# Gated recurrence: the guard of the gates' sum moved from an addition by ScalarE into the logarithm's bias and the refinement

## The chip, the cores and the metric

The kernel runs on one NeuronCore of a Trainium2 chip. The metric is the device time of one execution in microseconds (us), lower is better. Every engine (TensorE = PE, VectorE = DVE, ScalarE = ACT, GpSimd = POOL, SyncE = SP) runs its own list of instructions in order; between engines, and between dependent instructions of one engine, semaphores keep the order.

## What is computed

`x` is 16 sequences of 256 tokens with 256 features, fp32. Four residual layers follow each other: attention, a gated recurrence, a mixture of experts with a shared expert, and a tanh recurrence. The change lies in the second one, which the reference gives as

```python
EPS = 1e-08
forget_gate = sigmoid(x @ W_f.T + b_f)
input_gate = sigmoid(x @ W_i.T + b_i)
gate_sum = forget_gate + input_gate + EPS
forget_norm = forget_gate / gate_sum
input_norm = input_gate / gate_sum
candidate = x @ W_h.T + b_h
new_info = input_norm * candidate
log_ret = log(forget_norm + EPS)
log_cumprod = cumsum(log_ret, axis=1)
padded = concatenate([zeros, log_cumprod], axis=1)
scaling = exp(log_cumprod[:, -1:, :] - padded[:, :-1, :])
hidden = cumsum(scaling * new_info, axis=1)
hidden = hidden + exp(log_cumprod) * cond[:, None, :]
x = x + hidden
```

## The kernel before

`x` lies in SBUF with the features on the partitions (`XT`, 128 partitions x 2 halves of the features x 16 sequences x 256 tokens). The stage before the change is the attention (`attention`), the one after it the experts (`experts`); each is a block of its own, and the next begins when all engines have left the last.

`recurrence` (line 842) works in 16 units, numbered 0 to 15. Unit n is feature half n % 2 of the two sequences of pair n // 2: tiles of 128 x 512. All tiles (`fg`, `ig`, `ie`, `total`, `inv`, `keep`, `start`, `hid`) have two slots, n % 2. Each engine has a written order, and this sets who can wait for whom:

- TensorE (L887): for each unit the products of the input gate, then the forget gate, then the candidate, into the three parts of the PSUM tile `pg`. The candidate of unit n waits until `pn` of unit n - 2 is written (`new_ready`).
- ScalarE, per round: the two sigmoids of unit n + 1 (`ig` L899, `fg` L901), the addition of 1e-8 to the input gate (`ie` L903), a table load (L923), Ln of `total` (L908) and Exp of minus that (L910), which together give a first value of 1 / total in PSUM, a table load back (L911), and then for unit n `keep` = normalised forget gate + 1e-8 (L918). The sigmoid of a unit waits for `keep` two units before it.
- GpSimd, per round: `total` = fg + ie of unit n + 1 (L932), the two normalisations of unit n (`ig` L937, `fg` L938), the two additions to `XT` of unit n - 1 (L945, L947).
- VectorE, per round: `pn` = (candidate + bias) * normalised input gate of unit n (L979), one refinement of the reciprocal of unit n + 1 (L967, L970: with y the first value and s the total, (2 - s * y) * y), then for unit n six scans of 128 x 256 (L989, L991, L995, two each) and the product `hid` (L998). With a cumulative product of `keep` the scans replace the reference's logarithms.

`pn`, `pg` and the zeros of the scans (`pz`) lie in PSUM, the rest in SBUF.

Of the kernel before, what the change touches and what calls it, by code (L numbers as in the profile page):

```python
# [11 lines left out]
P = 128  # L12
# [829 lines left out]
def recurrence(nc, env):  # L842
    fp32, ALU, ACT = (env[k] for k in ("fp32", "ALU", "ACT"))
    sb, ps, sem, vec = (env[k] for k in ("sb", "ps", "sem", "vec"))
    XT, eps8, wfih = (env[k] for k in ("XT", "eps8", "wfih_sb"))
    N = 2 * T
    UNITS = B
    st = ExitStack()
    with st:
        fg = sb(st, "fg", [P, 2, N])  # L850
        ig = sb(st, "ig", [P, 2, N])
        ie = sb(st, "ie", [P, 2, N])
        total = sb(st, "total", [P, 2, N])
        inv = sb(st, "inv", [P, 2, N])
        keep = sb(st, "keep", [P, 2, N])
        after = sb(st, "after", [P, 2, T + 1])
        start = sb(st, "start", [P, 2, N])
        hid = sb(st, "hid", [P, 2, N])
        pg = [ps(st, f"pg{u}", [P, 3, N]) for u in range(2)]
        pn = ps(st, "pn", [P, N])  # L860
        pz = ps(st, "pz", [P, 512])
        constants, products, gates, summed, inverse, normed, kept, new_ready, scanned, hid_ready, added = (
            sem(st, n) for n in ("constants", "products", "gates", "summed", "inverse", "normed", "kept", "new_ready", "scanned",
                                 "hid_ready", "added"))
        i_products, f_products, log_ready, seed_ready, refined = (
            sem(st, n) for n in ("i_products", "f_products", "log_ready", "seed_ready", "refined"))
# [4 lines left out]
        def half(v, j):  # L871

            return v[:, j * T:(j + 1) * T]
# [17 lines left out]
        @block.scalar  # L891
        def _(act):
            def open_gates(n):
                u, q = n % 2, n % 2
                act.wait_ge(i_products, n + 1)
                if n >= 2:
                    act.wait_ge(new_ready, n - 1)
                    act.wait_ge(kept, n - 1)
                nc.scalar.activation(ig[:, q], pg[q][:, 1], ACT.Sigmoid, bias=vec("b_i", u, u + 1)).then_inc(gates, 1)  # L899
                act.wait_ge(f_products, n + 1)  # L900
                nc.scalar.activation(fg[:, q], pg[q][:, 0], ACT.Sigmoid, bias=vec("b_f", u, u + 1)).then_inc(gates, 1)  # L901
                act.wait_ge(gates, 3 * n + 1)
                nc.scalar.activation(ie[:, q], ig[:, q], ACT.Identity, bias=eps8[:, 0:1]).then_inc(gates, 1)  # L903

            def seed(n):
                q = n % 2
                act.wait_ge(summed, n + 1)
                nc.scalar.activation(pg[q][:, 1], total[:, q], ACT.Ln).then_inc(log_ready, 1)  # L908
                act.wait_ge(log_ready, n + 1)
                nc.scalar.activation(pg[q][:, 1], pg[q][:, 1], ACT.Exp, scale=-1.0).then_inc(seed_ready, 1)  # L910
                nc.scalar.preload_act_table_set("sigmoid_and_others")  # L911

            def add_eps(n):
                q = n % 2
                act.wait_ge(normed, 2 * n + 2)
                if n >= 2:
                    act.wait_ge(hid_ready, n - 1)
                nc.scalar.activation(keep[:, q], fg[:, q], ACT.Identity, bias=eps8[:, 0:1]).then_inc(kept, 1)  # L918

            for n in range(-1, UNITS):  # L920
                if n + 1 < UNITS:
                    open_gates(n + 1)
                    nc.scalar.preload_act_table_set("natural_log_exp_and_others")  # L923
                    seed(n + 1)
                if n >= 0:
                    add_eps(n)

        @block.gpsimd
        def _(pool):
            def add_gates(n):  # L930
                pool.wait_ge(gates, 3 * (n + 1))
                nc.gpsimd.tensor_tensor(total[:, n % 2], fg[:, n % 2], ie[:, n % 2], ALU.add).then_inc(summed, 1)  # L932

            def normalise(n):
                q = n % 2
                pool.wait_ge(inverse, n + 1)
                nc.gpsimd.tensor_tensor(ig[:, q], ig[:, q], inv[:, q], ALU.mult).then_inc(normed, 1)  # L937
                nc.gpsimd.tensor_tensor(fg[:, q], fg[:, q], inv[:, q], ALU.mult).then_inc(normed, 1)  # L938

            def add_to_x(n):  # L940
                p, u, q = n // 2, n % 2, n % 2
                pool.wait_ge(hid_ready, n + 1)
                pool.wait_ge(products, 2 * (p + 1))
                xv = XT[:, u, 2 * p:2 * p + 2]
                nc.gpsimd.tensor_tensor(xv, xv, start[:, q].rearrange("p (j t) -> p j t", j=2), ALU.add).then_inc(added, 1)  # L945
                pool.wait_ge(added, 2 * n + 1)
                nc.gpsimd.tensor_tensor(xv, xv, hid[:, q].rearrange("p (j t) -> p j t", j=2), ALU.add).then_inc(added, 1)  # L947

            add_gates(0)
            for n in range(UNITS):  # L950
                if n + 1 < UNITS:
                    add_gates(n + 1)
                normalise(n)
                if n > 0:
                    add_to_x(n - 1)
            add_to_x(UNITS - 1)

        @block.vector
        def _(dve):
            nc.vector.memset(zeros, 0.0).then_inc(constants, 1)  # L960
            nc.vector.memset(after[:, :, T:T + 1], 1.0).then_inc(constants, 1)
            dve.wait_ge(constants, 2)

            def invert(n):
                q = n % 2
                dve.wait_ge(seed_ready, n + 1)
                nc.vector.scalar_tensor_tensor(out=inv[:, q], in0=total[:, q], scalar=-1.0, in1=pg[q][:, 1],  # L967
                                               op0=ALU.mult, op1=ALU.mult).then_inc(refined, 1)
                dve.wait_ge(refined, n + 1)
                nc.vector.scalar_tensor_tensor(out=inv[:, q], in0=inv[:, q], scalar=2.0, in1=pg[q][:, 1],  # L970
                                               op0=ALU.add, op1=ALU.mult).then_inc(inverse, 1)

            def new_info(n):
                u, q = n % 2, n % 2
                dve.wait_ge(products, n + 1)
                dve.wait_ge(normed, 2 * n + 1)
                if n > 0:
                    dve.wait_ge(hid_ready, n)
                nc.vector.scalar_tensor_tensor(out=pn[:], in0=pg[q][:, 2], scalar=vec("b_h", u, u + 1), in1=ig[:, q],  # L979
                                               op0=ALU.add, op1=ALU.mult).then_inc(new_ready, 1)  # L980

            def scans(n):

                p, u, q = n // 2, n % 2, n % 2
                s = Steps(dve, scanned, 6 * n)
                dve.wait_ge(kept, n + 1)
                dve.wait_ge(new_ready, n + 1)
                for j in range(2):
                    s.op(nc.vector.tensor_tensor_scan(half(pn[:], j), half(pn[:], j), half(keep[:, q], j), 0.0, ALU.add, ALU.mult))  # L989
                for j in range(2):  # L990
                    s.op(nc.vector.tensor_tensor_scan(after[:, j, T - 1::-1], half(keep[:, q], j)[:, ::-1], zeros, 1.0, ALU.mult, ALU.add))  # L991
                if n >= 2:
                    dve.wait_ge(added, 2 * (n - 1))
                for j in range(2):
                    s.op(nc.vector.tensor_tensor_scan(half(start[:, q], j), half(keep[:, q], j), zeros, h0[:, u, 2 * p + j:2 * p + j + 1],  # L995
                                                      ALU.mult, ALU.add))
                dve.wait_ge(scanned, 6 * n + 4)
                nc.vector.tensor_tensor(hid[:, q].rearrange("p (j t) -> p j t", j=2), pn[:].rearrange("p (j t) -> p j t", j=2),  # L998
                                        after[:, :, 1:T + 1], ALU.mult).then_inc(hid_ready, 1)

            invert(0)
            for n in range(UNITS):
                new_info(n)
                if n + 1 < UNITS:
                    invert(n + 1)
                scans(n)
# [608 lines left out]
```

## Time and profile before

| | |
|---|---|
| median of 3 runs | 1357.46 us (1354.88 to 1358.3) |
| the profiled execution | 1354.25 us, its span 1352.5 us |
| PE busy | 1215.1 us (90%) |
| DVE busy | 883.2 us (65%) |
| ACT busy | 632.5 us (47%) |
| POOL busy | 329.9 us (24%) |

Times in views are us from the start of the span. In the timeline a row is an instruction (or several alike, xcount): its start, its duration, engine, line, operation, output and inputs, and in brackets the idle time of its engine ahead of it with what ended it. Idle time under about 0.2 us isn't printed. The recurrence lasts from 453.3 us (first product) to 573.9 us (first instruction of the experts).

### The profile page before, as it was taken

To read this page: it belongs to the slowest core of one execution; us is meant where nothing else is said; L and a number is where in the kernel's file an instruction comes from. 1 tells how busy PE (TensorE), PEld (TensorE's weight loads), DVE (VectorE), ACT (ScalarE), POOL (GpSimd) and SP (SyncE) were. 2 spreads that over 40 slices of the span, in tenths; PEclk is the share of its full clock that TensorE was granted. 3 is DMA by queue.
4 is the path that set the end of the run, shared out by engine and by line. 5 is a ranking of instruction groups with operands and counts; after the bars stand their busy time and mean duration, and the time that the engine had idled before them with its cause. 6 is when DMAs were issued, how large, how long until landed. Compare 5 with 4: busy or idle time off the path is not lost. (4 is left out here: it accounts for less than half of the span.)

```text
span 1352.5 us, 34667 instructions
## 1 busy us (share of the span) xinstructions
PE 1215.1 (90%) x14232; PEld 977.0 (72%) x14232; DVE 883.2 (65%) x2091; ACT 632.5 (47%) x1191; POOL 329.9 (24%) x311
## 2 busy tenths in 40 slices
PE   4389999999998888329999999999999999999995
PEld 2257676766665333129999999999988888888884
DVE  4978787887864399867666666666555555555552
ACT  2167777777766599612333333333233333333331
POOL 1554544444453299800000000000000000000000
PEclk9799999999999899759999999999999999999996
DMA  9212121211214000039999999999700000000000
GB/s 348 94 48 95 48 95 49 85 59 64 80 49 148 24 0 1 0 129 397 397 374 366 364 364 365 367 365 364 273 2 18 10 19 11 19 10 19 11 18 18
DMA packets 81196, 188.31 MB, mean 139 GB/s; under 512 B 4112, under 2 KB 14480, under 8 KB 80784
## 3 DMA queue, kind: packets, MB, share of 16 engines
q1 hardware_dynamic: 81040, 186.11, 38.1%
q8 instruction: 113, 1.85, 0.6%
q14 instruction: 43, 0.35, 0.1%
HBM read 160.66 MB, written 25.17 MB: 137 GB/s over the span
## 5 line engine op out<-in xcount | busy, mean ns | idle before, releaser
L1118 ACT ACTIVATE g<-ph,b 128x256 f32<-128x256 f32 x256 | 121.2, 474 | 248.3 <-PE ph L1282 248.3
L549 DVE TENSOR_REDUCE mx<-pR 128x4 f32<-128x1024 f32 x128 | 156.3, 1224 | 62.6 <-PE pR L707 61.2
L1499 DVE STREAM_TRANSPOSE preT<-pr 128x64 f32<-128x64 f32 x256 | 63.7, 249 | 163.7 <-PE pr L1392 163.2
L1280 PE MATMUL ph<-xhi,w 128*128 128x256 f32 x512 | 145.8, 285 | 13.2 <-DMA w<-weight_halves 13.2
L1226 DVE CAST ghi<-g 128x256 fp32r<-128x256 f32 x256 | 74.7, 292 | 126.6 <-ACT g L1118 126.4
L1474 ACT ACTIVATE hs<-preT 128x32 f32<-128x32 f32 x256 | 58.7, 229 | 199.6 <-DVE preT L1499 198.6
L1296 PE MATMUL py<-ghi,w 128*128 128x256 f32 x512 | 145.7, 285 | 1.7 <-DVE glo L1228 1.6
L1281 PE MATMUL ph<-xlo,w 128*128 128x256 f32 x512 | 145.7, 285 | 0.0
L1282 PE MATMUL ph<-xhi,w 128*128 128x256 f32 x512 | 145.7, 284 | 0.0
L1297 PE MATMUL py<-glo,w 128*128 128x256 f32 x512 | 144.9, 283 | 0.0
L1298 PE MATMUL py<-ghi,w 128*128 128x256 f32 x512 | 144.9, 283 | 0.0
L421 ACT ACTIVATE probs<-pR 128x1024 f32<-128x1024 f32 x128 | 129.3, 1024 | 22.6 <-PE pR L716 21.0
L1392 PE MATMUL pr<-wh_sb,hs 128*32 128x64 f32 x4096 | 114.0, 231 | 8.9 <-ACT hs L1474 8.9
L1228 DVE TENSOR_TENSOR glo<-g,ghi 128x256 fp32r<-128x256 f32 x256 | 108.9, 425 | 8.8
L1280 PEld LDWEIGHTS ph<-xhi,w 128*128 128x128 f32 x512 | 99.1, 193 | 13.5 <-issue 13.5
L1543 POOL TENSOR_TENSOR staged<-xc,hs 128x256 f32<-128x256 f32 x32 | 22.7, 732 | 347.5 <-ACT hs L1474 347.5
L1392 PEld LDWEIGHTS pr<-wh_sb,hs 128*32 128x32 f32 x4096 | 71.4, 112 | 46.1 <-ACT hs L1474 13.4
L887 PE MATMUL pg<-XT,wfih_sb 128*128 128x512 f32 x192 | 86.4, 600 | 17.1 <-DVE pn L979 15.9
L1296 PEld LDWEIGHTS py<-ghi,w 128*128 128x128 f32 x512 | 98.2, 192 | 3.4 <-DVE glo L1228 3.2
L1534 POOL MEMSET hs<- 128x2048 f32 x1 | 1.8, 1804 | 403.0 <-POOLq L1049 403.0
L1281 PEld LDWEIGHTS ph<-xlo,w 128*128 128x128 f32 x512 | 99.1, 194 | 0.0
L1282 PEld LDWEIGHTS ph<-xhi,w 128*128 128x128 f32 x512 | 99.1, 194 | 0.0
(195 smaller groups left out, 2973.0 us busy)
## 6 DMA issues: line engine op xcount, KB each, us to landing
w<-weight_halves SPq DMA_DIRECT2D x132, 1024.0 KB, 7.9
weight_halves<-wparts SPq DMA_DIRECT2D x40, 512.0 KB, 3.9
modw<-in_ew SPq DMA_DIRECT2D x32, 256.0 KB, 4.6
xn<-in_x_tok SPq DMA_DIRECT2D x4, 1024.0 KB, 11.7
XT<-in_x_dm SPq DMA_DIRECT2D x2, 2048.0 KB, 14.8
out_dm<-staged SPq DMA_DIRECT2D x16, 256.0 KB, 2.1
modw<-in_sw SPq DMA_DIRECT2D x8, 256.0 KB, 4.0
modw<-in_mod_w SPq DMA_DIRECT2D x1, 768.0 KB, 7.0
```

Source lines behind the costliest of these rows:

```text
L421: nc.scalar.activation(probs[:, j % 4], pR[k][:], ACT.Exp, scale=HD ** -0.5).then_inc(free[k], 1)
L549: nc.vector.reduce_max(mx[:, :, 2 * j:2 * j + 2].rearrange("p t s -> p s t"), pR[k][:].rearrange("p s (t k) -> p s t k", t=TC), AX.X).then ...
L887: i = nc.tensor.matmul(pg[n % 2][:, g], wfih[:, c, g * D + u * P:g * D + (u + 1) * P], XT[:, c, 2 * p:2 * p + 2], start=(c == 0), stop=(c ...
L1118: nc.scalar.activation(g[:, t % RING], ph[t % RING][:, 0:T], ACT.Gelu_apprx_tanh, bias=b1[:, n, f:f + 1]).then_inc(gelu_done, 1)
L1228: nc.vector.tensor_tensor(glo[:, t % RING], g[:, t % RING], ghi[:, t % RING].bitcast(fp32), ALU.subtract).then_inc(lo_done, 1)
L1280: nc.tensor.matmul(dst, whi, hi, start=(k == 0), stop=False)
L1281: nc.tensor.matmul(dst, whi, lo, start=False, stop=False)
L1282: i = nc.tensor.matmul(dst, wlo, hi, start=False, stop=(k == DC - 1))
L1296: nc.tensor.matmul(dst, whi, hi, start=(f == 0), stop=False)
L1297: nc.tensor.matmul(dst, whi, lo, start=False, stop=False)
L1298: i = nc.tensor.matmul(dst, wlo, hi, start=False, stop=(f == FC - 1))
L1392: i = nc.tensor.matmul(dst[QW * j:QW * (j + 1)], prev[:, c], quad(wh[:, c], j), start=False, stop=(c == DC - 1), skip_group_check=True)
```

## The change

Three edits. The addition by ScalarE (`ie`) goes, with its tile, and the guard 1e-8 is put where the sum is used: as the bias of Ln, an operand of 128 x 1 in the place of the plain 0, and as the scalar that is added to `total` in the first half of the refinement. GpSimd adds `fg` and `ig` and waits for two increments of `gates` per unit instead of three. Since the refinement's first half then has no place for the minus sign, it comes out as (s * y - 2) * y, the negative reciprocal; normalised `ig`, `fg`, `pn` and `hid` change their sign, `keep` takes it back by a scale of -1, and the last addition becomes a subtraction. The order on every engine is otherwise unchanged, and so is the number of instructions on TensorE, VectorE and GpSimd; ScalarE has 16 fewer.

```diff
@@ recurrence
-        ie = sb(st, "ie", [P, 2, N])
@@ open_gates(n), ScalarE
                 act.wait_ge(f_products, n + 1)
                 nc.scalar.activation(fg[:, q], pg[q][:, 0], ACT.Sigmoid, bias=vec("b_f", u, u + 1)).then_inc(gates, 1)
-                act.wait_ge(gates, 3 * n + 1)
-                nc.scalar.activation(ie[:, q], ig[:, q], ACT.Identity, bias=eps8[:, 0:1]).then_inc(gates, 1)
@@ seed(n), ScalarE
-                nc.scalar.activation(pg[q][:, 1], total[:, q], ACT.Ln).then_inc(log_ready, 1)
+                nc.scalar.activation(pg[q][:, 1], total[:, q], ACT.Ln, bias=eps8[:, 0:1]).then_inc(log_ready, 1)
@@ add_eps(n), ScalarE
-                nc.scalar.activation(keep[:, q], fg[:, q], ACT.Identity, bias=eps8[:, 0:1]).then_inc(kept, 1)
+                nc.scalar.activation(keep[:, q], fg[:, q], ACT.Identity, bias=eps8[:, 0:1], scale=-1.0).then_inc(kept, 1)
@@ add_gates(n), GpSimd
-                pool.wait_ge(gates, 3 * (n + 1))
-                nc.gpsimd.tensor_tensor(total[:, n % 2], fg[:, n % 2], ie[:, n % 2], ALU.add).then_inc(summed, 1)
+                pool.wait_ge(gates, 2 * (n + 1))
+                nc.gpsimd.tensor_tensor(total[:, n % 2], fg[:, n % 2], ig[:, n % 2], ALU.add).then_inc(summed, 1)
@@ add_to_x(n), GpSimd
-                nc.gpsimd.tensor_tensor(xv, xv, hid[:, q].rearrange("p (j t) -> p j t", j=2), ALU.add).then_inc(added, 1)
+                nc.gpsimd.tensor_tensor(xv, xv, hid[:, q].rearrange("p (j t) -> p j t", j=2), ALU.subtract).then_inc(added, 1)
@@ invert(n), VectorE
-                nc.vector.scalar_tensor_tensor(out=inv[:, q], in0=total[:, q], scalar=-1.0, in1=pg[q][:, 1],
-                                               op0=ALU.mult, op1=ALU.mult).then_inc(refined, 1)
+                nc.vector.scalar_tensor_tensor(out=inv[:, q], in0=total[:, q], scalar=1e-8, in1=pg[q][:, 1],
+                                               op0=ALU.add, op1=ALU.mult).then_inc(refined, 1)
                 dve.wait_ge(refined, n + 1)
                 nc.vector.scalar_tensor_tensor(out=inv[:, q], in0=inv[:, q], scalar=2.0, in1=pg[q][:, 1],
-                                               op0=ALU.add, op1=ALU.mult).then_inc(inverse, 1)
+                                               op0=ALU.subtract, op1=ALU.mult).then_inc(inverse, 1)
```

## Rows read from the trace of the kernel before

**Rows 1.** Steady stretch: length, busy PE, PEld, DVE, ACT, POOL, PEclk, DMA share, GB/s.
```profile
500.00:533.00 33.00, 27.09 (x60) 10.99 (x60) 31.10 (x51) 31.65 (x41) 30.99 (x26) 1.00 0.00 0
```

**Rows 2.** Timeline of ScalarE, one round (sigmoids of unit 14, `keep` of unit 13).
```profile
547.38 0.72 ACT L918 ACTIVATE keep<-fg,eps 128x512 f32<-128x512 f32 x1
548.22 0.69 ACT L899 ACTIVATE ig<-pg,small 128x512 f32<-128x512 f32 x1
548.80 0.68 ACT L901 ACTIVATE fg<-pg,small 128x512 f32<-128x512 f32 x1
549.37 0.72 ACT L903 ACTIVATE ie<-ig,eps 128x512 f32<-128x512 f32 x1
550.11 1.28 ACT L923 ACT_TABLE_LOAD   x1
551.47 0.60 ACT L908 ACTIVATE pg<-total 128x512 f32<-128x512 f32 x1
552.10 0.58 ACT L910 ACTIVATE pg<-pg 128x512 f32<-128x512 f32 x1
552.70 1.28 ACT L911 ACT_TABLE_LOAD   x1
554.00 0.72 ACT L918 ACTIVATE keep<-fg,eps 128x512 f32<-128x512 f32 x1
```

**Rows 3.** Timeline of GpSimd, the round that begins with `total` of unit 15.
```profile
556.78 1.26 POOL L932 TENSOR_TENSOR total<-fg,ie 128x512 f32<-128x512 f32 x1 [0.34 <-ACT ie L903]
558.01 1.26 POOL L937 TENSOR_TENSOR ig<-ig,inv 128x512 f32<-128x512 f32 x1
...
563.01 1.26 POOL L937 TENSOR_TENSOR ig<-ig,inv 128x512 f32<-128x512 f32 x1
```

**Rows 4.** Timeline of VectorE, from `pn` of unit 13 to the last `hid`.
```profile
552.77 0.76 DVE L979 SCALAR_TENSOR_TENSOR pn<-pg,small,ig 128x512 f32<-128x512 f32 x1 [0.34 <-POOL ig L937]
...
559.37 0.76 DVE L979 SCALAR_TENSOR_TENSOR pn<-pg,small,ig 128x512 f32<-128x512 f32 x1 [0.33 <-POOL ig L937]
560.03 0.68 DVE L967 SCALAR_TENSOR_TENSOR inv<-total,pg 128x512 f32<-128x512 f32 x1
560.75 0.69 DVE L970 SCALAR_TENSOR_TENSOR inv<-inv,pg 128x512 f32<-128x512 f32 x1
561.36 1.28 DVE L989 TENSOR_TENSOR_SCAN pn<-pn,keep 128x256 f32<-128x256 f32 x2
...
564.98 0.66 DVE L998 TENSOR_TENSOR hid<-pn,after 128x512 f32<-128x512 f32 x1
565.79 0.76 DVE L979 SCALAR_TENSOR_TENSOR pn<-pg,small,ig 128x512 f32<-128x512 f32 x1
...
570.27 0.66 DVE L998 TENSOR_TENSOR hid<-pn,after 128x512 f32<-128x512 f32 x1
```

**Rows 5.** Timeline of the first two units, ScalarE, and the first `pn` of VectorE.
```profile
457.60 0.71 ACT L903 ACTIVATE ie<-ig,eps 128x512 f32<-128x512 f32 x1
...
463.36 0.72 ACT L903 ACTIVATE ie<-ig,eps 128x512 f32<-128x512 f32 x1
...
466.76 0.76 DVE L979 SCALAR_TENSOR_TENSOR pn<-pg,small,ig 128x512 f32<-128x512 f32 x1 [4.35 <-POOL ig L937]
```

**Rows 6.** Timeline of TensorE, a candidate product of the recurrence.
```profile
553.58 1.98 PE L887 MATMUL pg<-XT,wfih_sb 128*128 128x512 f32 x4 [1.20 <-DVE pn L979]
```

**Rows 7.** Waits in the recurrence: who waited for whom, us in total, times, longest.
```profile
POOL total L932 <- ACT ie L903: 29.6, 16, 18.0
```

**Rows 8.** Busy time and clock by stretch (columns as in rows 1), start of the experts.
```profile
604.00:606.00 2.00, 2.00 (x10) 1.77 (x9) 0.57 (x2) 1.71 (x3) 0.00 (x0) 0.50 1.01 375
606.00:608.00 2.00, 1.76 (x13) 1.49 (x12) 1.76 (x9) 0.55 (x2) 0.00 (x0) 1.00 1.05 420
```

**Rows 9.** Durations (ns, min/median/max) of one line of VectorE and one of GpSimd.
```profile
L989 DVE TENSOR_TENSOR_SCAN pn<-pn,keep x32: 671/683/699, 468.7 to 567.3; 128x256 f32<-128x256 f32 x32
L945 POOL TENSOR_TENSOR XT<-XT,start x16: 1257/1272/1286, 474.4 to 571.0; 128x512 f32<-128x512 f32 x16
```

## The prediction

> **What bounds the stage now.** I first read the busy time by stretch: in the steady part of the recurrence ScalarE (31.65 of 33 us), VectorE (31.10) and GpSimd (30.99) are all nearly full, TensorE is not [rows 1]. Three engines at 94 to 96% can't be told apart by busy time, so I went on to the timelines, to see which one never waits. On ScalarE a round takes 554.00 - 547.38 = 6.62 us and no row shows a wait [rows 2]. GpSimd waits 0.34 us per round, and what ends the wait is `ie` of ScalarE, the instruction that the change removes [rows 3]. VectorE waits 0.33 us per round for the normalised `ig` of GpSimd [rows 4], TensorE 1.20 us for `pn` of VectorE [rows 6]. So the chain of waits runs TensorE <- VectorE <- GpSimd <- ScalarE, and ScalarE's own order closes the loop. From the first `pn` at 466.76 to the fifteenth (unit 14) at 559.37 [rows 5, 4] there are 14 rounds of 6.615 us.
>
> **What a round would take without ScalarE.** The gain is not what ScalarE loses, but the distance to the next bound. Each engine's own round can be read:
>
> - ScalarE: starts of `fg`, `ie` and the table load are 0.57 and 0.74 us apart [rows 2]. Without `ie` the load follows `fg` (0.68 us long) as it followed `ie`, 0.02 us after its end, so 0.70 us after `fg` started instead of 1.31: 0.61 us less, taken as 0.60. `total` can start earlier by the same. ScalarE's round is then 6.0 us.
> - GpSimd: after unit 15's `total` (556.78) it runs five operations without a wait, up to the next `ig` at 563.01 [rows 3], where no `total` stands any more. That is `total`, `ig`, `fg` and two additions, just a round's worth: 6.23 us.
> - VectorE: `pn` of unit 15 starts with no printed wait. At that point GpSimd's `ig` had been finished since 563.01 + 1.26 = 564.27, and ScalarE's work of the unit was over, so this is VectorE on its own: 565.79 - 559.37 = 6.42 us [rows 4, 3]. The round is that long although the idle time taken away is 0.33 us (6.615 - 0.33 would be 6.28), because `hid` ends at 565.64 and `pn`, which also waits for it, starts 0.15 us later, whereas earlier this gap lay hidden in the wait.
> - TensorE: idle for 1.20 of 6.62 us, so 5.42 us.
>
> The longest is VectorE's 6.42. So the round falls from 6.615 to 6.42, by 0.195 us, and not by 0.60.
>
> **The change part by part.**
>
> 1. `ie` removed, steady part: 14 rounds x 0.195 = **-2.73 us**. The other 0.4 us of each `ie` becomes idle time of ScalarE. What is late next is VectorE itself; GpSimd and ScalarE then run ahead of it until the wait for `hid` (`add_to_x`) or for `pn` (the sigmoids) holds them.
> 2. `ie` removed, fill: ahead of the first `pn` stands `total` of unit 1, because GpSimd adds the gates of unit 1 before it normalises unit 0. On the way there ScalarE works through both units alone, so both `ie` (457.60 and 463.36) count whole [rows 5]: 2 x 0.60 = **-1.20 us**.
> 3. The bias of Ln. The trace has no Ln with such an operand. Nearest rows: Ln without it 0.60, Exp 0.58, the sigmoids with one 0.68 and 0.69 (they too have one end in PSUM), the identity with one, SBUF on both ends, 0.72 [rows 2]. So it costs 0 to 0.12 us per Ln; I take 0.09, since the sigmoids are the nearest. In the steady part it is covered: ScalarE's round of 6.09 us, with 0.12 even 6.12, is under 6.42. In the fill Ln of unit 0 lies on the path (**+0.09**), and Ln of unit 1 delays `keep` of unit 0, which ends just as the scans are due: in unit 13, which stands for unit 0 here, `keep` ends at 554.00 + 0.72 = 554.72 [rows 2], and the scans follow `pn` by 561.36 - 559.37 = 1.99 us, thus 552.77 + 1.99 = 554.76 [rows 4]: **+0.09**. In later rounds VectorE is the slower of the two, and `keep` is early. The bounds are 0 and 0.24 for both together. ScalarE: Activation LUTs, section What ACT_TABLE_LOAD costs, in the Trainium skill, prices a bias operand of 128 x 1 at about 93 ns against an immediate one. With that price the sum would be -3.74 instead of -3.75; no row here shows it for an Ln.
> 4. Refinement: an add in the place of a multiply (L967), a subtract in the place of an add (L970). L970, which has an add, takes 0.69, L967 with two multiplies 0.68 [rows 4]: between 0 and +0.01 x 16, **0**. The bound of 0.16 us matters as VectorE is the new bound.
> 5. Scale -1 on `keep` (Exp has such a scale and takes 0.58 [rows 2]), a subtraction on GpSimd instead of an addition: **0**. Their cover, if they cost 0.1 us each, is the 0.3 us that ScalarE and the 0.2 us that GpSimd have left per round.
> 6. After the recurrence the two additions of unit 15, the hand-over to the experts, the gating, the fetch of the experts' weights and their products follow from the last `hid`. Nothing in them depends on absolute time, so they move forward whole: **0**, with one reserve. TensorE enters the experts at a granted clock of 0.50 (1.2 GHz), after it had been idle for most of the time since 555.6 us, and has 1.00 (2.4 GHz) from 606 on [rows 8]. Where this change falls could shift against the work; I allow ±1 us, half of a row of 2 us at either side.
>
> Sum: -2.73 - 1.20 + 0.18 = **-3.75 us**. The profiled execution, 1354.25 us around a span of 1352.5, would go to 1350.5. It stands 3.2 us below the median of the runs, 1357.46; applied to the median the sum gives 1353.7 us. That is 0.28% less, and a measurement of this kernel can tell about 0.3% (4.1 us) from no change.
>
> **The rivals.**
>
> - **GpSimd is the next bound, not VectorE.** If the 0.15 us between `hid` and `pn` belonged to the end of the stage alone, VectorE's round would be near 6.28 and GpSimd's is 6.23, so the round 6.25 or so. For it: ordinary gaps of VectorE are smaller (560.03 + 0.68 to 560.75 is 0.04 us [rows 4]). Against it: unit 15 has the same instructions in the same order. 14 x 0.365 + 1.02 = 6.1 us: 1351.3. Chance 0.12.
> - **ScalarE's addition was not on the loop.** The 1.2 us of the fill comes, but the loop is held by something beside it (the load and the wait for `keep`, for example), so that rounds stay at 6.6: gain 1.0 us, 1356.5. Against it: the wait of GpSimd ended by `ie` in all 16 rounds [rows 7]. Chance 0.10, with the case that the change costs in Ln what it saves.
> - **The experts start at an unlucky moment of the clock.** The gain is halved, 1355.5. Chance 0.12.
> - **Slower: GpSimd and VectorE get into each other's way.** Now both run against each other in fixed phase. After the change GpSimd drifts ahead of VectorE until the wait for `hid` stops it, and other pairs of operations meet. If one VectorE instruction per round had to wait for a whole GpSimd operation (1.27 us), the round would be 6.42 + 1.27 = 7.69 and the stage 14 x 1.075 - 1.0 = 14 us longer: 1371.5. It decides from 0.27 us per round on, where gain and loss cancel. Against it: in the steady part both are busy 94% of the time, thus overlap in nearly every instruction, and the 32 scans still take 671 to 699 ns, the 16 additions 1257 to 1286 [rows 9]. Chance 0.03. SBUF — State Buffer, section Who interferes with whom, in the Trainium skill, says that a VectorE instruction with two SBUF inputs and a GpSimd instruction that reads SBUF exclude each other for their whole length. Here every VectorE instruction of the round has one input in PSUM, so by that rule the rival would not come, and the narrow durations agree.
>
> **How the numbers follow.** Chance of the forecast (round set by VectorE, 6.3 to 6.45 us) 0.63, GpSimd 0.12, no loop gain 0.10, clock 0.12, slower 0.03. The predicted time is the forecast's, 1353.7 us. The unknown costs give it -0.2 to +0.3, the clock ±1. The range goes down to the GpSimd case with some scatter, 1350.5, and up to the case without a loop gain, 1357.0; beyond it are the slow case and the edges of the others. The forecast lies just short of 4.1 us, so with its scatter of about 1 us and a median that moves as much, I give it 0.28 of faster by over 0.3% and 0.35 of within; the GpSimd case is faster, 0.12; the two cases with a lesser gain are within, 0.20 of 0.22; the slower one is slower. Faster 0.41, within 0.3% 0.56, slower 0.03.
>
> **What would show it.** In the timeline of the changed kernel: no `ie`; starts of `fg` and of the table load 0.70 us apart; first `pn` about 1.1 us earlier than 466.76 where the recurrence starts at the same time; rounds of 6.42 us from `pn` to `pn` with no printed wait ahead of `pn`; ScalarE waiting some 0.3 us per round for `pn` or for GpSimd in the later units; Ln at 0.69; TensorE idle for about 1.0 us. The forecast is wrong if the round is below 6.3 or above 6.5, if durations of VectorE or GpSimd grow, or if the time from the last `hid` to the end of the span differs from 1352.5 - 570.93 = 781.6 us [rows 4] by more than 1 us.

## The result and the profile after

| | before | changed |
|---|---|---|
| median of 22 runs | 1358.8 us (1354.88 to 1363.58) | 1355.2 us (1351.15 to 1359.61) |
| ratio to before, 95% interval | | 0.9972 (0.9959 to 0.9985) |
| profiled execution, its span | 1354.25, 1352.5 | 1353.02, 1351.2 |
| recurrence, from ScalarE's first table load to the experts' first VectorE instruction | 453.26 to 573.97: 120.71 | 457.90 to 574.62: 116.72 |
| ahead of it | 453.26 | 457.90 |
| behind it | 778.53 | 776.58 |

The change saves 0.28% of the time by the ratio, which is 3.8 us, with an interval from 0.15 to 0.41% (2.0 to 5.6 us); the medians differ by 3.6 us. A single execution doesn't show that well: the two profiled spans differ by 1.3 us only. Cut at the borders of the stage they do. The recurrence is 3.99 us shorter; the attention ahead of it, whose code is the same in both, took 4.64 us longer in this execution, and what lies behind 1.95 us less. Where those two come from is told at the end; for the change only the stage counts.

The timeline of VectorE in the changed kernel, where line numbers are three lower than before (`pn` is L976, the refinement L964 and L967, `hid` L995), begins with the first two `pn`:

```profile
470.27 0.76 DVE L976 SCALAR_TENSOR_TENSOR pn<-pg,small,ig 128x512 f32<-128x512 f32 x1 [3.73 <-POOL ig L934]
...
476.77 0.76 DVE L976 SCALAR_TENSOR_TENSOR pn<-pg,small,ig 128x512 f32<-128x512 f32 x1
...
501.58 0.66 DVE L995 TENSOR_TENSOR hid<-pn,after 128x512 f32<-128x512 f32 x1
502.39 0.76 DVE L976 SCALAR_TENSOR_TENSOR pn<-pg,small,ig 128x512 f32<-128x512 f32 x1
503.06 0.68 DVE L964 SCALAR_TENSOR_TENSOR inv<-total,pg 128x512 f32<-128x512 f32 x1
503.77 0.69 DVE L967 SCALAR_TENSOR_TENSOR inv<-inv,pg 128x512 f32<-128x512 f32 x1
...
508.80 0.76 DVE L976 SCALAR_TENSOR_TENSOR pn<-pg,small,ig 128x512 f32<-128x512 f32 x1
```

Where [rows 4] had `0.34 <-POOL ig` ahead of each `pn`, nothing is printed now: VectorE shows no wait for another engine (a wait under about 0.2 us would not be printed; `dve_more` below settles it). Its round is 508.80 - 502.39 = 6.41 us (6.405 over 14 rounds) instead of 6.615, the duration of the refinement is as before, and `hid` to `pn` is 0.81 us from start to start, as it was ahead of unit 15 only. The first round is longer, 6.50.

ScalarE's timeline of the same stretch answers to [rows 2]:

```profile
502.70 0.72 ACT L915 ACTIVATE keep<-fg,eps 128x512 f32<-128x512 f32 x1
503.54 0.69 ACT L898 ACTIVATE ig<-pg,small 128x512 f32<-128x512 f32 x1
504.12 0.68 ACT L900 ACTIVATE fg<-pg,small 128x512 f32<-128x512 f32 x1
504.82 1.28 ACT L920 ACT_TABLE_LOAD   x1
506.34 0.69 ACT L905 ACTIVATE pg<-total,eps 128x512 f32<-128x512 f32 x1 [0.23 <-POOL total L929]
507.06 0.58 ACT L907 ACTIVATE pg<-pg 128x512 f32<-128x512 f32 x1
```

`ie` is gone, the load starts 0.70 us after `fg`, Ln takes 0.69 instead of 0.60, and ScalarE now waits for GpSimd's sum. GpSimd in turn runs ahead of VectorE at first. Its sums start 6.26 us apart up to 511.31, and 6.40 us apart from there on, where the addition of `start` follows the end of `hid` by 0.08 us (515.06 and 515.14):

```profile
498.78 1.27 POOL L929 TENSOR_TENSOR total<-fg,ig 128x512 f32<-128x512 f32 x1
505.04 1.27 POOL L929 TENSOR_TENSOR total<-fg,ig 128x512 f32<-128x512 f32 x1
...
549.73 1.27 POOL L929 TENSOR_TENSOR total<-fg,ig 128x512 f32<-128x512 f32 x1
556.13 1.26 POOL L929 TENSOR_TENSOR total<-fg,ig 128x512 f32<-128x512 f32 x1
```

So this trace shows both rounds at once: GpSimd's own, 6.26 us, and VectorE's, 6.405. Four of the waits of the recurrence in the changed kernel, whole stage (who waited for whom, us in total, times, longest); the view names no `ie` and no repeated wait on VectorE:

```profile
POOL total L929 <- ACT fg L900: 24.8, 3, 18.5
PE pg L886 <- DVE pn L976: 12.4, 13, 1.0
ACT pg L905 <- POOL total L929: 4.1, 13, 0.4
DVE pn L976 <- POOL ig L934: 3.7, 1, 3.7
```

### The profile page after: what moved, and what is told of

It is laid out like the page before. It is cut to its first block and busy times, and to the rows that moved or that the text cites. A ratio compares the mean times of both kernels' runs of the same rounds, so it can differ in the third digit from the quotient of the medians.

```text
span 1351.2 us, 34651 instructions
## 1 busy us (share of the span) xinstructions
PE 1219.9 (90%) x14232; PEld 979.4 (72%) x14232; DVE 883.0 (65%) x2091; ACT 624.3 (46%) x1175; POOL 330.0 (24%) x311
## 5 line engine op out<-in xcount | busy, mean ns | idle before, releaser
L1294 PEld LDWEIGHTS py<-glo,w 128*128 128x128 f32 x512 | 98.4, 192 | 0.0
```

The lines of the kernel that those rows point to most:

```text
L1294: nc.tensor.matmul(dst, whi, lo, start=False, stop=False)
```

## The experiments

The stage's length, its first `pn` (counted from the table load that opens it) and its rounds are read from one profile each. They repeat well: `pe_order`, which differs from the changed kernel only in the order of TensorE's products, gave the same 116.72 us, and the first `pn` came at 12.37 in five profiles. (`split_adds` is the exception and is explained there; `before` and the changed kernel both had TensorE at a granted clock of 1.00 in the first 4 us of the stage.) The time of an execution wanders by some 4 us to either side, so the stage is the measure except where a ratio is given.

| kernel | first pn | round | stage |
|---|---|---|---|
| before | 13.50 | 6.615 | 120.71 |
| changed | 12.37 | 6.405 | 116.72 |
| ie_back | 12.90 | 6.63 | 120.91 |
| ie_back_waited | 13.58 | 6.705 | 122.15 |
| exp_bias | 12.45 | 6.405 | 116.87 |
| dve_more | 12.37 | 6.62 | 119.94 |
| pool_more | 12.37 | 6.41, from the sixth on 6.50 | 117.71 |
| pe_order | 12.37 | 6.405 | 116.72 |
| in_place | 12.37 | 6.17, from the fourth on 6.255 | 114.20 |
| split_adds | 13.87 | 6.17 | 114.15 |

### Was ScalarE the loop? ie_back and ie_back_waited

```diff
 # ie_back, against the changed kernel: ie computed, read by nobody
                 nc.scalar.activation(fg[:, q], pg[q][:, 0], ACT.Sigmoid, bias=vec("b_f", u, u + 1)).then_inc(gates, 1)
+                act.wait_ge(gates, 2 * n + 1)
+                nc.scalar.activation(ie[:, q], ig[:, q], ACT.Identity, bias=eps8[:, 0:1])
 # ie_back_waited, against ie_back: the sum waits for it
-                act.wait_ge(gates, 2 * n + 1)
-                nc.scalar.activation(ie[:, q], ig[:, q], ACT.Identity, bias=eps8[:, 0:1])
+                act.wait_ge(gates, 3 * n + 1)
+                nc.scalar.activation(ie[:, q], ig[:, q], ACT.Identity, bias=eps8[:, 0:1]).then_inc(gates, 1)
...
-                pool.wait_ge(gates, 2 * (n + 1))
+                pool.wait_ge(gates, 3 * (n + 1))
```

> The addition ie is put back on ScalarE alone, in its old place between the sigmoids and the table load; nothing reads it, GpSimd's sum doesn't wait for it, and the rest of the change stays. If ScalarE's own order was the loop (the prediction's reading), its round is 6.62 us of before plus 0.09 for the bias of Ln: rounds of 6.70 to 6.71 us from pn to pn, no wait on ScalarE, GpSimd waiting for ScalarE again, first pn at 13.5 + 0.1 us after the table load that opens the stage less what the early sum saves (none: the sigmoid of unit 1 is late by ie of unit 0; ie of unit 1 isn't in the way), so 13.0. Rival, that what held the kernel was only GpSimd's wait for ie: rounds stay at 6.41.

Measured: rounds of 6.63, first `pn` 12.90. The first round was longer, 7.04, since the scans of unit 0 waited 0.5 us for `keep`, which `ie` of unit 1 had delayed. The rival (6.41) is out: with `ie` on ScalarE alone the stage is as long as before (120.91 us against 120.71). But 6.63 isn't 6.70, so ScalarE's own order was not quite the loop. Its timeline shows what differs:

```profile
508.74 0.72 ACT L903 ACTIVATE ie<-ig,eps 128x512 f32<-128x512 f32 x1
509.46 1.28 ACT L923 ACT_TABLE_LOAD   x1
510.76 0.69 ACT L908 ACTIVATE pg<-total,eps 128x512 f32<-128x512 f32 x1
```

Here Ln follows the load by 510.76 - (509.46 + 1.28) = 0.02 us. In [rows 2] it is 551.47 - 551.39 = 0.08, too short for a printed wait: Ln waited for GpSimd's sum, which could only start after `ie`. That gave the second kernel:

> As ie_back, which had rounds of 6.63 us, but GpSimd's sum waits for ie again, as before the change. Theory now: the loop of before wasn't ScalarE's order alone, it went from ie over GpSimd's sum (0.06 + 1.27 + 0.04 us) to Ln, 0.07 us longer than the table load beside it (1.28 + 0.03); so 6.615 = 6.54 + 0.07, and 6.63 = 6.54 + 0.09 of Ln's bias. Then rounds are 6.70 here. Rival, that the sum plays no part and the bias costs nothing in a round: 6.63 again.

Measured: 6.705. VectorE waits 0.34 us in each round, as before the change, and GpSimd 0.41 instead of 0.34. So the loop of before ran `ig`, `fg`, `ie`, over GpSimd's sum, Ln, Exp, load, `keep`. ScalarE's order by itself comes to 6.54 us. No kernel ran with it alone; it is 6.63 less the 0.09 of Ln's bias, and also 6.615 less the 0.07 that the way over the sum is longer than the load, and the two agree. The first `pn` at 13.58 also settles the fill: `ie` of unit 0 on ScalarE delayed it by 0.53 us (`ie_back`), and the wait for both `ie` by another 0.68, 1.21 us together.

### The price of the bias: exp_bias

```diff
-                nc.scalar.activation(pg[q][:, 1], pg[q][:, 1], ACT.Exp, scale=-1.0).then_inc(seed_ready, 1)
+                nc.scalar.activation(pg[q][:, 1], pg[q][:, 1], ACT.Exp, bias=eps8[:, 0:1], scale=-1.0).then_inc(seed_ready, 1)
```

> The changed kernel with the same 128x1 operand as bias of Exp as well (1e-8 is added to the exponent). Ln went from 602 to 692 ns with it. Theory: Exp goes from 582 to about 672 ns, ScalarE's round from about 6.09 to 6.18, which VectorE's 6.405 still covers: rounds of 6.405, the first pn 0.09 us later, and keep of unit 0 another 0.09 behind the scans that need it: stage longer by 0.15 to 0.2 us in all. Rival, that ScalarE has no room left: rounds grow by 0.09, the stage by 1.4 us.

One line of ScalarE in the changed kernel (Ln) and one in this (Exp), durations in ns, min/median/max:

```profile
L905 ACT ACTIVATE pg<-total,eps x16: 691/692/693, 463.7 to 557.4; 128x512 f32<-128x512 f32 x16
```

```profile
L907 ACT ACTIVATE pg<-pg,eps x16: 662/662/664, 463.2 to 557.1; 128x512 f32<-128x512 f32 x16
```

Ln went from 602 to 692 ns, Exp from 582 to 662. Rounds stayed at 6.405; the first `pn` came 0.08 later and the first round took 6.58 instead of 6.50: the stage is 0.15 us longer in all. So the operand costs 0.08 to 0.09 us each time, and in the steady part it is covered. The first round of the changed kernel, 0.095 longer than the others, is the same effect of Ln's bias: `keep` of unit 0 is late by it.

### Which engine is the bound now: dve_more and pool_more

```diff
 # dve_more, VectorE, in each round ahead of scans(n)
+                nc.vector.memset(spare[:], 0.0)
 # pool_more, GpSimd, in each round ahead of the wait of add_gates(n)
+                nc.gpsimd.memset(spare[:, n], 0.0)
```

> The changed kernel with one more VectorE instruction per round, a memset of a spare 128x256 tile in SBUF ahead of the scans (a memset of that size into PSUM took 0.27 us). Theory, VectorE is the bound in every round: rounds grow by the start to start time of the new instruction, 0.20 to 0.27 us, to 6.60 to 6.68, and the stage by 3 to 4 us. Rival, GpSimd or a loop through it is the bound: rounds grow by 0.15 us less than the instruction, or not at all.

Measured: rounds of 6.62. The memset lasts 0.27 us and each round grows by 0.22, as expected for VectorE as the bound; the rival, with GpSimd as the bound, expected 0.15 us less than the instruction. Only the first round grows less (6.50 to 6.62), because there the scans had to wait for `keep` anyway.

> The changed kernel with one more GpSimd instruction per round, a memset of a spare 128x256 tile ahead of the sum (by the kernel's other memsets, 204 ns for 128x128 and 1804 for 128x2048, about 0.3 us). Theory: GpSimd's own round is 6.25 to 6.26 and has 0.15 us of room under VectorE's 6.405; with 0.27 to 0.31 us more it becomes the bound, rounds of 6.52 to 6.57, VectorE waiting for it ahead of pn again. Rival, that GpSimd is covered by more than that: rounds stay at 6.41.

Measured: four rounds of 6.40 to 6.41 after the first, then 6.50 to 6.52. GpSimd's timeline:

```profile
558.75 0.31 POOL L929 MEMSET spare<- 128x256 f32 x1
559.02 1.26 POOL L931 TENSOR_TENSOR total<-fg,ig 128x512 f32<-128x512 f32 x1
```

The memset lasts 0.31 us, but the sum follows it 0.27 us later and the round grew to 6.50, a little less than expected. With 0.10 us per round above VectorE's 6.405, GpSimd first uses up the lead it had, and then holds `pn` up. With its own round of 6.26 in the changed kernel it stood 0.15 us per round under VectorE, and the next gain on VectorE ends there.

### Taking VectorE's gap away: in_place and pe_order

In `in_place`, `pn` is written over the candidate in `pg`, so `new_info` needs no wait for `hid` of the unit before; TensorE has to compute the candidate later.

```diff
 # VectorE
-                if n > 0:
-                    dve.wait_ge(hid_ready, n)
-                nc.vector.scalar_tensor_tensor(out=pn[:], in0=pg[q][:, 2], ...
+                nc.vector.scalar_tensor_tensor(out=pg[q][:, 2], in0=pg[q][:, 2], ...
 # scans and hid read pg[q][:, 2] in the place of pn
 # TensorE
+            for n in range(UNITS + 1):
+                if n < UNITS:
+                    product(n, 1, i_products)
+                    product(n, 0, f_products)
+                if n > 0:
+                    product(n - 1, 2, products)
 # product(n, 2) waits for hid_ready n - 1 (pe_order: new_ready n - 1, as before)
```

> The changed kernel with pn written over the candidate in pg instead of into a bank of its own, so that new_info needs no wait for hid of the unit before; TensorE computes the candidate of a unit after the input and forget products of the next one, and waits for hid two units before. Theory, that the gap of 0.15 us between hid and pn is this wait: pn starts about 0.6 us after hid instead of 0.81, VectorE's own round falls to 6.2, GpSimd's 6.25 to 6.26 becomes the bound: rounds of 6.26, stage shorter by 14 x 0.15 = 2.1 us against the changed kernel, 0.15% of the time. Rival, that the gap is something else (PSUM, the end of a strided operation): rounds stay at 6.41. Second rival: the later candidate products hold pn up: rounds above 6.41.

Measured: ratio to the kernel before 0.9939 (0.9916 to 0.9961). That interval still touches the changed kernel's (0.9959 to 0.9985), so the further gain rests on the stage. The stage is 114.20 us, 2.5 us shorter than the changed kernel's. VectorE's timeline:

```profile
501.86 0.66 DVE L998 TENSOR_TENSOR hid<-pg,after 128x512 f32<-128x512 f32 x1
502.44 0.75 DVE L979 SCALAR_TENSOR_TENSOR pg<-pg,small,ig 128x512 f32<-128x512 f32 x1
```

Without the wait `pn` starts 0.58 us after `hid` and overlaps its end, where it was 0.81. VectorE's own round is 6.17 (second and third round); from then on GpSimd sets it at 6.255. The expectation counted 0.15 us for fourteen rounds; the first three, in which GpSimd still had its lead, gained 0.23 each, hence 2.5 and not 2.1.

> The changed kernel with the in-place variant's order on TensorE alone (candidate products of a unit after the input and forget products of the next), pn in its own bank and the wait for hid ahead of it kept. Theory, that the gain of the in-place variant (rounds 6.25, early ones 6.17) came from the wait for hid: rounds stay at 6.405. Rival, that it came from TensorE's order: rounds of 6.25.

Measured: rounds of 6.405, stage 116.72, first `pn` 12.37. TensorE's order changes nothing by itself, so the gain is that of `pn` in place. That takes the wait away and also lets `pn` be written to another PSUM tile; a kernel with only the wait gone wasn't run, so that it is the wait, and not the tile, is argued and not shown apart.

### Relieving GpSimd too: split_adds

```diff
 # GpSimd, against in_place: add_to_x taken apart (VectorE's waits for free slots of start and hid likewise)
+            def add_start(n):
+                pool.wait_ge(scanned, 6 * (n + 1))
+                ...
+            def add_hid(n):
+                pool.wait_ge(hid_ready, n + 1)
+                pool.wait_ge(start_added, n + 1)
+                ...
                 normalise(n)
-                if n > 0:
-                    add_to_x(n - 1)
-            add_to_x(UNITS - 1)
+                if n > 1:
+                    add_hid(n - 2)
+                if n > 0:
+                    add_start(n - 1)
+            add_hid(UNITS - 2)
+            add_start(UNITS - 1)
+            add_hid(UNITS - 1)
```

> The in-place variant (rounds 6.25) with GpSimd's two additions to XT taken apart: start is added when its scans are done, hid one round later, so that no addition waits for the one just ahead of it (gap of 0.13 us per round), and of the tail behind the last hid only one addition remains instead of two. Theory: GpSimd's round falls to 6.12, VectorE's own 6.17 to 6.18 becomes the bound, 12 rounds x 0.08 = 1.0 us, and the tail 1.35 us: stage 2.3 us shorter than the in-place variant's 114.2 us. Rival, that GpSimd isn't the bound there: only the tail's 1.35 us.

Measured: ratio to the kernel before 0.9943 (0.9922 to 0.9963), not to be told from `in_place`. The rounds are 6.17 as expected, so GpSimd was the bound in `in_place`. The tail was wrong: from the last `pn` to the experts it is 7.66 us instead of 8.17, a gain of 0.5 and not 1.35. GpSimd's timeline at the end:

```profile
569.00 1.26 POOL L948 TENSOR_TENSOR XT<-XT,start 128x512 f32<-128x512 f32 x1 [1.62 <-DVE start L1005]
570.41 1.26 POOL L955 TENSOR_TENSOR XT<-XT,hid 128x512 f32<-128x512 f32 x1
```

The addition of `start` waits for its scans, which end only one VectorE instruction ahead of `hid`, so the addition of `hid` still queues behind it. From the first `pn` to the experts `split_adds` takes 100.28 us, `in_place` 101.83. That its whole stage is no shorter comes from the first `pn`, 1.50 us later in this execution, though the edit leaves the order of everything ahead of it as it was. The first sigmoid waited 2.25 us for TensorE's products, in the changed kernel 0.75 (table load at 457.87 and 457.90):

```profile
461.40 0.69 ACT L904 ACTIVATE ig<-pg,small 128x512 f32<-128x512 f32 x1 [2.25 <-PE pg L885]
```

```profile
459.94 0.69 ACT L898 ACTIVATE ig<-pg,small 128x512 f32<-128x512 f32 x1 [0.75 <-PE pg L886]
```

In the first 2 us of the stage TensorE was granted 0.50 (1.2 GHz) in `split_adds` and 1.00 (2.4 GHz) in all the other nine profiles. Over the longer stretch around it, in `split_adds` and in the changed kernel (columns as in [rows 1]; only TensorE's matter):

```profile
450.00:462.00 12.00, 8.93 (x18) 5.13 (x19) 2.13 (x6) 2.47 (x3) 0.00 (x0) 0.54 0.01 1
```

```profile
450.00:462.00 12.00, 8.89 (x22) 5.18 (x23) 2.17 (x6) 2.90 (x4) 0.00 (x0) 0.71 0.01 1
```

## Why the prediction was right

It gave -3.75 us, 1353.7 us and a chance of 0.56 for a difference within 0.3%; measured were -3.8 us by the ratio (-3.6 by the medians), 1355.2 us and 0.28%. The median is above the forecast because that of the kernel before, with more runs, was 1358.8 and not 1357.46. That the totals meet to 0.1 us is luck, as the interval goes from 2.0 to 5.6 us. What bears the prediction out is the stage, -3.99 us, part by part:

1. Steady part, -2.73 forecast. Against 14 rounds of 6.615 and one of 6.42 (99.03 us) stand one of 6.50 and 14 of 6.405 (96.17 us): -2.86, which already holds the +0.09 of `keep` of unit 0. Without it -2.95. The rest, 0.2 us, is that VectorE's own round is 6.405, while the one round that showed it before was 6.42. The choice to take the round of unit 15, and not 6.615 less the printed idle time (6.28), decided the forecast: 6.28 would have given 2 us more.
2. Fill, -1.20 + 0.09 forecast, measured 12.37 - 13.50 = -1.13. Right to 0.02 us, and for the reason given: the two `ie` put back cost 1.21 us (13.58 - 12.37).
3. Bias of Ln, 0.09 per Ln taken between 0 and 0.12: 602 to 692 ns. ScalarE: Activation LUTs, section What ACT_TABLE_LOAD costs, in the Trainium skill, gives about 93 ns for such an operand. The trace agrees for Ln (90 ns); Exp, with 80 ns, is a little below.
4. Refinement, sign and subtraction, 0: VectorE's 0.68 and 0.69 stand, and GpSimd's operations take 1.26 to 1.28 as before.
5. Tail of the stage, 0: 8.18 us from the last `pn` to the experts in both.

**What it had wrong.** The sentence that ScalarE's own order closes the loop: the loop ran over GpSimd's sum, and ScalarE alone was 6.54 us (worked out from `ie_back`). Hence ScalarE's round after the change, put at 6.09, is about 6.54 - 0.61 + 0.09 = 6.02. The step from 6.615 wasn't hurt, since only the distance to the next bound counted, but a 0.08 us gap that the timeline doesn't print should have been worked out. Of what then holds whom, GpSimd running ahead until `hid` stops it came true; ScalarE is held by GpSimd's sum (0.23, later 0.38 us per round), where point 1 of the prediction named `pn` and its signs `pn` or GpSimd.

The last of the signs of a wrong forecast came up although the forecast held: the time from the end of the last `hid` to the end should stay within 1 us of 781.6 us. It is 1351.2 - (570.92 + 0.67) = 779.6 us, 2.0 less. The prediction looked for the clock's effect at the start of the experts, within 1 us; the 2 us lie at the end of the routed experts. Of the ten profiles, five were granted 0.80 to 0.84 from 401 to 406 us behind the end of the recurrence, and their time behind the stage is 778.3 to 778.5 us (`before`, `exp_bias`, `ie_back`, `pe_order`, `split_adds`). The other five were granted 1.00 there, and theirs is 776.6 to 777.1 (the changed kernel, `dve_more`, `in_place`, `pool_more`, `ie_back_waited`). Both groups have kernels with the change, so this is no effect of it. Whether the kernel before also takes both values isn't known, as it has one profile.

The rivals: GpSimd as the bound (6.25) is out, as VectorE pays for each instruction more; a round that stays at 6.6 is out; VectorE and GpSimd slowing each other is out, since their durations stand (scans 670 to 699 ns, additions to `XT` 1260 to 1280, against [rows 9]) although both are now busy 97 to 98% of the steady part:

```profile
500.00:533.00 33.00, 28.06 (x64) 11.48 (x63) 32.11 (x53) 30.29 (x37) 32.29 (x28) 1.00 0.00 1
```

The rival of the clock at the start of the experts can't be separated for this change in particular, but it is small: within each of the two groups above the time behind the stage differs by 0.2 and 0.5 us.

## What to carry to other kernels

Where three engines are each busy 94% of a stage, what a removed instruction gains is the distance to the second longest round, and that is best read from a round in which the present bound is already out of the way, at the end of the stage for example; the round less the printed idle time is too short, because a wait also hides the gaps of the engine's own dependences. Here 0.60 us taken from ScalarE gave 0.21 us per round. After such a step look for the new bound's own waits: an in-place tile that made one wait needless gave another 0.15 to 0.24 us per round, and each such gain ends at the next engine, 0.15 us away.

## What was not expected

**A wait for the instruction just ahead costs 0.12 to 0.23 us here.** `hid` to `pn` is 0.81 us from start to start with the wait and 0.58 without it (but see `in_place` for what else changed). The two additions to `XT` on GpSimd, the second waiting for the first, are 1.34 to 1.36 us apart, independent ones 1.23 (`split_adds`). In the refinement it is less than 0.23 too: L964 starts 0.09 us before the end of `pn`, on which it doesn't wait (502.39 + 0.76 against 503.06), and L967 starts 0.03 us after the end of L964, on which it does, a difference of 0.12. Why `pn`, with three waits in a row, pays more than the others wasn't tried.

**The scatter of the executions goes with TensorE's granted clock.** Over the 22 runs of the changed kernel the mean clock is between 0.948 and 0.958, and the correlation with the time is -0.96: the six runs above 1358 us had 0.948 to 0.950, the one of 1351.15 had 0.958. The profiles show stretches where the granted clock differs. From 70 to 80 us, in the attention, the kernel before (first row) was granted 1.00 (2.4 GHz) and the changed one (second) 0.59:

```profile
70.00:80.00 10.00, 6.28 (x33) 3.49 (x34) 8.08 (x9) 4.68 (x7) 6.21 (x6) 1.00 0.00 0
```

```profile
70.00:80.00 10.00, 8.64 (x26) 4.07 (x24) 4.54 (x5) 3.37 (x5) 6.21 (x6) 0.59 0.00 0
```

Over ten profiles the recurrence began between 453.3 and 460.9 us. The earliest two, `before` (453.3) and `ie_back_waited` (454.1), had 1.00 in this stretch; the latest, `dve_more`, had 0.50. This stretch isn't all of it: `exp_bias` had 1.00 too and began at 456.7, `pe_order` had 0.68 and began at 456.3. In the other direction, from 975 to 980 us, at the end of the routed experts, the kernel before was granted 0.80 and the changed one 1.00:

```profile
975.00:980.00 5.00, 3.25 (x19) 2.95 (x18) 1.17 (x4) 0.47 (x1) 1.98 (x3) 0.80 0.02 3
```

```profile
975.00:980.00 5.00, 3.28 (x27) 2.98 (x26) 1.71 (x6) 0.47 (x1) 1.89 (x3) 1.00 0.01 3
```

Read at the same distance behind the recurrence, this stretch divides the ten profiles into the two groups named above, about 2 us apart. The attention and the experts are the same code in all ten, so a single execution of this kernel can't tell 4 us from nothing, while the length of one stage between two of its own instructions can. Why the clock rises earlier in one execution than in another stays open; no run here was made for it.
